# Two graph layers on one core: the second layer gathers its rows as three bf16 pieces in place of one fp32 row

## The reference

```python
def _rgcn_layer(x, src, dst, edge_type, w_rel, root, bias):
    seg = dst * NUM_REL + edge_type                     # NUM_REL = 10
    xs = x[src]                                         # (200000, 128)
    sums = segment_sum(xs, seg, num_segments=N * NUM_REL)
    cnt = segment_sum(ones(seg.shape), seg, num_segments=N * NUM_REL)
    mean = (sums / maximum(cnt, 1.0)[:, None]).reshape(N, NUM_REL, -1)
    return einsum('nrd,rdo->no', mean, w_rel) + x @ root + bias

edge_type = argmax(msg[:, 16:-16], axis=1)              # msg is (200000, 42)
h = relu(_rgcn_layer(x, src, dst, edge_type, w_rel1, root1, b1))
y = _rgcn_layer(h, src, dst, edge_type, w_rel2, root2, b2)
return _layernorm(x + y)
```

## Time and profile before

| | |
|---|---|
| time, median of 3 runs | 4696.83 us (4691.28 to 4699.89) |
| the profiled execution: its time | 4687.58 us |
| the profiled execution: its span, first to last instruction | 4685.9 us |
| PE busy | 2460.3 us, 53% |
| DVE busy | 1878.4 us, 40% |
| POOL busy | 2994.9 us, 64% |
| mean granted TensorE clock | 0.716 of 2.4 GHz |
| layer 1, first to last gather | 0 to 2292.7 us |
| layer 2, first to last gather | 2361.75 to 4619.9 us |

### The profile page before, as it was taken

The page is one execution under the profiler, slowest core; times in us unless marked ns, Lnnn a source line. Parts: engine busy times, 40 slices in busy tenths (PEclk is TensorE's granted clock), DMA queues, the critical chain, the costliest instruction groups (busy, mean ns, idle before and its releaser), DMA issues.

```text
span 4685.9 us, 32483 instructions
## 1 busy us (share of the span) xinstructions
PE 2460.3 (53%) x10851; PEld 1795.0 (38%) x10852; DVE 1878.4 (40%) x2158; ACT 365.3 (8%) x397; POOL 2994.9 (64%) x3139
## 2 busy tenths in 40 slices
PE   3556566655656655565724454454445454544446
PEld 2344344443434444443523333333333333333334
DVE  4444444444444344444513333333333333333334
ACT  1001000010100001010100000010100000000100
POOL 7666666666666666666356666666666666666662
PEclk8677677676767667676766677777767676777777
DMA  4222222222222222222111222121212222221221
GB/s 117 61 62 80 62 65 75 63 79 61 80 62 63 77 61 79 63 74 57 41 48 49 55 53 56 51 59 52 56 53 56 54 55 54 56 56 52 56 55 34
DMA packets 147439, 285.98 MB, mean 61 GB/s; under 512 B 61147, under 2 KB 81711, under 8 KB 143824
## 3 DMA queue, kind: packets, MB, share of 16 engines
q0 software_dynamic: 100032, 205.07, 16.7%
q1 hardware_dynamic: 42604, 79.64, 5.2%
q10 hardware_dynamic: 4759, 0.73, 0.1%
HBM read 263.37 MB, written 21.85 MB: 61 GB/s over the span
## 4 chain that ended last, share of the span: by engine, by line
another core or an unknown queue 47%; DVE 20%; PE 18%; issue 11%; DVEq 3%; ACT 1%; DMA 0%; ACTq 0%; SPq 0%
PE ps_agg L1765 8%; DVE S L2103 6%; PE ps_out L1829 5%; DVE ring L2116 5%; DVE mean L2160 2%; DVE z_end L2141 2%; PE ps_bc L1783 2%; DVEq L2215 2%; PE ps_agg L1760 1%; DVEq L2112 1%; DVE hit L2097 1%; ACT ring L1596 1%; PE ps_out L1824 1%; DVEq L2116 0%
## 5 line engine op out<-in xcount | busy, mean ns | idle before, releaser
L1379 POOL DMA_INDIRECT rows<-table,idx_s x1563 | 1486.0, 951 | 841.2 <-issue 457.2
L1379 POOL DMA_INDIRECT rows<-in_x_dram,idx_s x1507 | 1449.1, 962 | 765.9 <-issue 446.9
L1765 PE MATMUL ps_agg<-S,rows 128*128 128x130 f32 (+3 forms) x6256 | 1527.2, 384 | 275.6 <-issue 274.6
L1765 PEld LDWEIGHTS ps_agg<-S,rows 128*128 128x128 f32 x6256 | 1239.9, 239 | 494.1 <-issue 415.1
L2116 DVE TENSOR_TENSOR ring<-ps_agg,ring 128x429 f32 (+1 forms) x782 | 456.3, 584 | 1889.0 <-remote 1459.0
L2103 DVE TENSOR_TENSOR S<-ps_iota,comb_b 128x1600 f32<-128x1600 f32 x392 | 712.5, 1818 | 108.4 <-issue 106.7
L1760 PE MATMUL ps_agg<-zero_b 128*128 128x429 bf16 (+1 forms) x782 | 321.9, 412 | 742.6 <-issue 385.5
L1783 PE MATMUL ps_bc<-rc_b,sel 74*128 74x448 bf16 x540 | 203.0, 469 | 908.3 <-DVE mean L2160 516.7
L2160 DVE TENSOR_TENSOR mean<-ps_bc,ring 128x896 f32<-128x896 f32 (+2 forms) x284 | 300.9, 1061 | 751.0 <-remote 692.3
L1829 PE MATMUL ps_out<-mean,wall 128*128 128x448 f32 (+1 forms) x1120 | 550.4, 620 | 55.9 <-DVE mean L2160 40.2
L1760 PEld LDWEIGHTS ps_agg<-zero_b 128*128 128x128 bf16 x782 | 88.8, 114 | 877.3 <-issue 628.5
(11 more groups left out here) (148 smaller groups left out, 645.2 us busy)
## 6 DMA issues: line engine op xcount, KB each, us to landing
attr<-in_edge_attr_dram SPq DMA_DIRECT2D x27, 1176.0 KB
rows<-table,idx_s POOLq DMA_INDIRECT x1563
rows<-in_x_dram,idx_s POOLq DMA_INDIRECT x1507
x_in<-in_x_dram SPq DMA_DIRECT2D x54, 224.0 KB
table<-h_s SPq DMA_DIRECT2D x27, 224.0 KB
table<-outT SPq DMA_DIRECT2D x27, 224.0 KB
xt_s<-table SPq DMA_DIRECT2D x27, 224.0 KB
out_dram<-h_s SPq DMA_DIRECT2D x27, 224.0 KB
```

The costliest lines, as they stand in the source:

```text
L1379: pool.indirect_dma_start(out=rows[:, o, j, :], out_offset=None, in_=(x, htab)[l][:, :], in_offset=bass.IndirectOffsetOnAxis(ap=at, axis=0 ...
L1765: ins = t_.matmul(sums[:, :, lo:lo + w], lhsT=rows[:, o, jj, :], rhs=S[:, (par + o) % 2, jj, :].rearrange("p (r n) -> p r n", n=WN)[:, :, ...
```

## The change

Layer 1 writes each row of `h` as three bf16 vectors of 128, a + b + c, that sum to the fp32 value: a is `h` rounded to bf16, b what is left rounded, c what is left then. A row of `htab` has 768 bytes in place of 512. Layer 2 gathers such rows and multiplies each piece by the same window of `S`, now in bf16 (its entries are 0 and 1), with fp32 accumulation. The cutting is new work in layer 1: ACT's copy of a half's rows now writes piece a only, and three instructions of DVE follow (`pieces`), the last of which raises `h_ready` in ACT's place. Some buffers share memory that they didn't share before, to make room; this adds no instruction.

```diff
-        rows = sb("rows", [P, OCTS, GT, C])
-        S = sb("S", [P, 2, GT, TCOL])
+        rows_h = sb("rows_h", [P, OCTS, GT, 3 * C], BF16)
+        rows_x = rows_h[:, :, :, 0:2 * C].bitcast(F32)
+        S_x = sb("S_x", [P, 2, GT, TCOL])
+        S_h = S_x[:, :, :, 0:TCOL // 2].bitcast(BF16)
...
+        h3_s = sb("h3_s", [NH, 4, 3 * C], BF16)
...
-        htab = table2[0:N, :]
+        htab = table2[0:3 * N // 2, :].rearrange("r c -> (r c)").bitcast(BF16).rearrange("(n d) -> n d", d=3 * C)
...
-                    out=rows[:, o, j, :], out_offset=None, in_=(x, htab)[l][:, :],
+                    out=(rows_x, rows_h)[l][:, o, j, :], out_offset=None, in_=(x, htab)[l][:, :],
...
-                    a_.copy(blocks(to, n).rearrange("p c d -> p (c d)"), bank[0:p, 0:c * C]).then_inc(h_ready, 1)
+                    a_.copy(blocks(to, n)[:, :, 0:C], bank[0:p, 0:c * C].rearrange("p (c d) -> p c d", c=c)
+                            ).then_inc(h_piece[0], 1)
...
-                        ins = t_.matmul(sums[:, :, lo:lo + w], lhsT=rows[:, o, jj, :],
-                                        rhs=S[:, (par + o) % 2, jj, :].rearrange("p (r n) -> p r n", n=WN)[:, :, 0:w],
-                                        start=False, stop=(j == 3 and l == 1))
+                        at = (S_x, S_h)[l][:, (par + o) % 2, jj, :].rearrange("p (r n) -> p r n", n=WN)[:, :, 0:w]
+                        for k in range((1, 3)[l]):
+                            ins = t_.matmul(sums[:, :, lo:lo + w],
+                                            lhsT=(rows_x, rows_h)[l][:, o, jj, k * C:(k + 1) * C], rhs=at,
+                                            start=False, stop=(j == 3 and l == 1 and k == 2))
...
+                def pieces(b, n, made, to, rest, bank=ps_out):
+
+                    to, rest = blocks(to, n), blocks(rest, n)
+                    p, c, _ = rest.shape
+                    dve.wait_ge(h_piece[0], made)
+                    hold(b)
+                    v_.tensor_tensor(rest, bank[0:p, 0:c * C].rearrange("p (c d) -> p c d", c=c), to[:, :, 0:C],
+                                     ALU.subtract).then_inc(h_piece[1], 1)
+                    dve.wait_ge(h_piece[1], made)
+                    v_.tensor_copy(to[:, :, C:2 * C], rest).then_inc(h_piece[2], 1)
+                    dve.wait_ge(h_piece[2], made)
+                    v_.tensor_tensor(to[:, :, 2 * C:3 * C], rest, to[:, :, C:2 * C], ALU.subtract
+                                     ).then_inc(h_ready, 1)
...
-                                if l == 1:
+                                if l == 0:
+                                    pieces(END - 1, HN, past, h3_s, h_s)
+                                else:
                                     centre(END - 1, HN, END, END - 1, past, (x_in_done, before * 16))
...
+                            if l == 0 and some and o == 5 and not last:
+                                pieces(b - 1, HN, past, h3_s, h_s)
+                            if l == 0 and last and o == 4:
+                                pieces(END, EARLY, end, h3_early, rest_end)
...
                     if l == 0:
+                        pieces(END, LATE, late, h3_late, rest_end, late_back)
```

More of the change, by code:

```diff
@@ L1195, in gnn_kernel @@
         back_turned = sem("back_turned")
+        h_piece = [sem(f"h_piece{k}") for k in range(3)]
         h_ready = sem("h_ready")
@@ L1248, in gnn_kernel @@
         first_q = sb("first_q", [1, QUADS])
-        row_u = sb("row_u", [1, 3 * QUADS])
         pos_i = sb("pos_i", [1, QUADS], I32)
@@ L1274, in gnn_kernel @@
         rc_m = sb("rc_m", [R, HN], BF16)
-        rising = mean[:, :, :].rearrange("p r n -> p (r n)")[:, 0:CHUNKS * P].rearrange("p (k c) -> p k c", c=P)
+        mean_f = mean[:, :, :].rearrange("p r n -> p (r n)")
+        rising = mean_f[:, 0:CHUNKS * P].rearrange("p (k c) -> p k c", c=P)
+        row_u = mean_f[0:1, CHUNKS * P:CHUNKS * P + 3 * QUADS]
+        half_row, lap_row, low_row, high_row = (
+            mean_f[0:1, CHUNKS * P + k * QUADS:CHUNKS * P + (k + 1) * QUADS] for k in range(3, 7))
         wall = [sb(f"wall{l}", [P, R, C]) for l in range(2)]
@@ L1291, in gnn_kernel @@
         outT_end = spare[:, 0:ENDN]
-        h_early = spare[0:EARLY // 2, 512:512 + 2 * C].rearrange("p (c d) -> p c d", c=2)
+        h3_early = spare[0:EARLY // 2, 512:512 + 3 * C].bitcast(BF16).rearrange("p (c d) -> p c d", c=2)
+        h3_late = z_end[:, 0:3, :].rearrange("p c d -> p (c d)").bitcast(BF16).rearrange("p (c d) -> p c d", c=2)
+        rest_end = spare[0:LATE // 2, 1536:1536 + 2 * C].rearrange("p (c d) -> p c d", c=2)
         sq_s = spare[0:NH, 768:768 + 4 * C].rearrange("p (c d) -> p c d", c=4)
@@ L1512, in _ @@
                         save_counts(b - 1, before)
-                        save_part(b - 1, 0, HN, before, h_s)
-                save_part(*EARLY_PART, PARTS - 1, h_early)
-                save_part(*LATE_PART, PARTS, z_end)
+                        save_part(b - 1, 0, HN, before, h3_s)
+                save_part(*EARLY_PART, PARTS - 1, h3_early)
+                save_part(*LATE_PART, PARTS, h3_late)
                 save_counts(END, PARTS)
@@ L1679, in _ @@
                                 take_out(l, b - 1, 0, HN, None if is_(b, 1) else prev, past, saved)
-                                take_rows(b - 1, HN, past, saved, h_s)
+                                take_rows(b - 1, HN, past, saved, h3_s)
                             else:
@@ L1695, in _ @@
                         take_out(l, *EARLY_PART, None, early, None)
-                        take_rows(END, EARLY, early, None, h_early)
+                        take_rows(END, EARLY, early, None, h3_early)
                         clear(0, HN, early - 1)
                         take_out(l, *LATE_PART, None, late, None, late_out)
-                        take_rows(END, LATE, late, None, z_end, late_back)
+                        take_rows(END, LATE, late, None, h3_late, late_back)
                         clear(1, ENDN, late)
@@ L2098, in take_types, with make_S @@
                                      bc(rel_t[:, cols], HT, WN), ALU.is_equal).then_inc(typ_taken, 1)
-                def make_S(par, o, used, sl):
+                def make_S(l, par, o, used, sl):
                     if used is not None:
                         dve.wait_ge(used[0], used[1])
-                    v_.tensor_tensor(S[:, sl, :, :], bc1(ps_iota[:, 0:TCOL], GT, TCOL),
+                    v_.tensor_tensor((S_x, S_h)[l][:, sl, :, :], bc1(ps_iota[:, 0:TCOL], GT, TCOL),
                                      bc(comb_b[:, par, o * GT:(o + 1) * GT], GT, TCOL), ALU.is_equal
@@ L2203, in _ @@
                 dve.wait_ge(comb_ready, 1)
-                make_S(0, 0, None, 0)
+                make_S(0, 0, 0, None, 0)
                 for l in range(2):
@@ L2234, in _ @@
                                 used = (agg_ready[o - 1], with_it) if o else (agg_ready[OCTS - 1], before)
-                                make_S(par, o + 1, None if l == 0 and is_(b, 0) and o == 0 else used, sl)
+                                make_S(l, par, o + 1, None if l == 0 and is_(b, 0) and o == 0 else used, sl)
                             elif not last:
@@ L2242, in _ @@
                                 hold(b)
-                                make_S(1 - par, 0, (agg_ready[o - 1], with_it), sl)
+                                make_S(l, 1 - par, 0, (agg_ready[o - 1], with_it), sl)
                             if some and o in (1, 2, 3):
@@ L2289, in _ @@
                     if l == 0:
+                        pieces(END, LATE, late, h3_late, rest_end, late_back)
                         dve.wait_ge(comb_in, 1)
-                        make_S(0, 0, (agg_ready[OCTS - 2], HALVES), 0)
+                        make_S(1, 0, 0, (agg_ready[OCTS - 2], HALVES), 0)
                     else:
```

7 lines of the change are left out of this document (2 added, 5 removed).

## The result

The changed kernel takes 4719.65 us (median of 5, 4711.74 to 4724.57), the one before 4694.82 us beside it (median of 5, 4691.28 to 4699.89). The ratio is 1.0049, 95% interval 1.0034 to 1.0064: slower, by some 23 us. The prediction (4692, within 4662 to 4760) had the time in its range and the direction wrong; "slower" had a chance of 0.28. The profiled execution took 4724.08 us, 36.5 us more than that of before.

A forecast was written before the change was run, and what follows sets the result against it. POOL's gather issue, with stalls for late signals, was taken as the bound, hardly depending on PE's speed. Terms -10.7 + 3 + 5.3 - 3 = -5.4 us on 4687.58 gave 4682, stated as 4692 for the median; range 4662 to 4760.

The forecast's parts named there:

- TensorE in layer 2: Layer 2's quads: three bf16 matmuls for one fp32 shorten PE's work, -10.7 us; bounds 0 and -20.
- 0.06 us for one: Both layers' loops: each us of PE or DVE work per 56 gathers costs 0.06 us, from the layers' difference.
- The relief: PE in layer 2: 0.44 us saved a quad at mean clock 0.71, 6.2 us in each half of 14 quads.
- The extra weight loads: PE in layer 2: taken as hidden beside matmuls; laid bare by 0.05 us each, twelve would eat the saving.
- Gathers of 768 bytes: POOL's gathers in layer 2: larger rows cost 0; upper bound +195 us.
- the rival of the larger rows: Layer 2's gathers: each holds up the next by up to 0.125 us, 4887; a third of that 4757; chance 0.15.
- Splitting in layer 1: DVE in layer 1's loop: calls of `pieces`, 2.0 us each, 26 times, cost +3 us; laid bare, +52.
- bare `pieces`: Layer 1: each call pushes the next octet out of DVE's burst, costing 52 us in place of 3, 4741; chance 0.10.
- Between the layers: Stage between the layers: splitting on DVE's chain and a larger store delay the first gather, +5.3 us; bounds 1.5 and 7.
- The larger store: SP's store of the LATE rows before layer 2's first gather: half as large again, +0.2 us.
- After the last gather: End of layer 2: eleven quads still to come, 0.28 us less each, -3 us; bounds 0 and -6.
- Relief counting for more: Layer 2: PE's shorter work lengthens stretches between stalls, giving back 56 us, 4647; half of it 4669; chance 0.22.

The follow-up runs named there:

- the bytes' kernel: Kernel before with layer 2's rows stored and gathered at 768 bytes, first 512 h in fp32, no splitting; 4687.05 us (0.9991) on chip 6.
- the paced kernel: Kernel before with two semaphore increments on POOL after each gather, meant to slow issue, which they didn't; 0.9996 of the kernel before on chip 1.

## Why the prediction was wrong

- **TensorE in layer 2: -10.7 us, measured +25.4 in the profiled pair (+16 on chip 6 against the bytes' kernel).** This is the step that failed. The pitch of a quad was nearly right (1.77 us at half clock for 1.67, 0.92 at full for 0.86). What was wrong is "That is 1.15 us for 18.7 us of work, 0.06 us for one": I put the difference between the layers down to busy time, where the same rows also show 5959 matmuls in layer 1 and 4375 in layer 2. The changed kernel makes layer 2's count that of layer 1, and its rate became layer 1's: 2282.6/1562 = 1.461 us a gather, for layer 1's 1.465 before. Had I put the whole difference down to the count, would have given (1.465 - 1.445) x 1563 = +31 us for this term, an estimate after the fact and above what was measured. My bounds, 0 and -20, let no loss in at all, although layer 1 stood there as a quad of 26 instructions with a slower rate. The relief itself was mis-sized too: 6.2 us a half would be 173 in layer 2, and TensorE's busy time fell by 13, and by 61 on chip 1 (1071 for the paced kernel's 1133), where there are no single steps. In both pairs the granted clock fell with the work, 0.71 to 0.67 and 0.77 to 0.72; I had kept it at 0.71.
- **The extra weight loads.** I had asked only whether they show beside the matmuls at full flow, and there they add little (0.92 us a quad for 0.86). The Trainium skill (TensorE: Matmul & The Clock Gate, LDWEIGHTS) made the term about 0 by their duration; that was nearer than my -10.7. The duration of the loads is not the reason either, since layer 2 took the same 2277 to 2278 us with loads busy for 893 us as for 677.
- **Gathers of 768 bytes: 0, measured 0 to +4 us.** The bytes' kernel has layer 2 at 2262.3 us for 2258.2 in the first profile of before, and as a whole it is 0.9991 of the kernel before on its own chip. A gather takes 951 ns, and the DMA share is 0.28 (0.29 said). That excludes the rival of the larger rows at the sizes it was given. By the fit of the Trainium skill (DMA: Bandwidth & Descriptors, Anatomy of one DMA) the further 32 KB of a gather are an estimated 0.075 us. If they took that, it lay under POOL's 1.25 us here.
- **Splitting in layer 1: +3, measured +7.4, and +9 to +14 on chip 6.** Right in sign, sized by the same 0.06 us for one; each call of 2.0 us cost 0.3 to 0.55. Stretches of 16 gathers in layer 1 went from 41 to 60, which the prediction had named as the sign of bare `pieces`; the cost stayed far below that rival's 52. On the chips of 4.00 ms it costs nothing.
- **Between the layers: +5.3, measured +7.8, +6.2 on chip 6 and +6.4 on chip 1.** The chain was right: transposes, spreads, EARLY, LATE, store. So were the terms of DVE: in the profiled pair the spreads come 2.6 us later against the start of the reciprocals, and the store 1.25 later behind ACT's copy. The larger store was mis-sized: from SP's issue to the first gather 5.75 us for 4.53 (5.72 for 4.55 on chip 1), +1.2 where I had 0.2.
- **After the last gather: -3, measured -4.1 in the pair but +4.8 on chip 6 against the bytes' kernel.** I costed the quads' pitch and left out that more broken quads can leave a longer backlog. The two measurements differ in sign, so the runs don't fix this term.
- **The rivals.** Relief counting for more was wrong in sign for the reason of the first point. None of my rivals was the one that came, more instructions at a price of their own. With the +31 from above it would have given 31 + 3 + 5.3 - 3 = +36 us, 4724 for the profiled execution, which took 4724.08; that the two agree so closely is luck, since the terms miss by 1 to 6 us each and the execution is a high one. That 4719.65 lies in the stated range is luck as well: the room above was made for larger rows and bare `pieces`, not for what came.

What the runs don't show: why a quad with more instructions is broken more often; whether fewer than 26 bf16 instructions would give the time back where signals are late; and whether loads, matmuls or both have the price.

## What to carry to other kernels

Where an engine's rows show single short instructions a fixed time apart, with nothing that ends the wait, count its instructions before you count its microseconds: turning one fp32 matmul into three bf16 ones took a fifth off an unbroken quad, and layer 2 lost 15 to 25 us with half as many passes and loads again. When two stages of a kernel differ in rate, list everything in which they differ; I took the one that I was looking for. And run the kernel before beside every experiment, on the same chip: here the quicker chips took 15% less, and on them this change cannot be measured.
